# Mixing as three products of rounded and rest parts, by units of 256 columns, in the spectral stage of a two-layer kernel

## The reference, cut to what matters

```python
U_plus, U_minus = _stu_conv(phi, u, n)        # causal convolutions with each filter, of u and of u * (-1)^t
out = einsum('btkd,k,kde->bte', U_plus, s, Mpp) + einsum('btkd,k,kde->bte', U_minus, s, Mpm)
# once for each prefix T, T/2, T/4, T/8 with its own matrices; the four results are summed with weights
```

## Time and profile before

| | us |
|---|---|
| median of 3 runs (lowest, highest) | 6383.73 (6379.6, 6387.01) |
| profiled execution | 6381.82 |
| its span, first to last instruction | 6379.8 |
| PE busy in the span | 5717.1 (90%) |
| DVE, ACT, POOL busy | 4526.8, 3160.5, 2768.9 |

### The profile page before, as it was taken

How to read it: one execution, slowest core, us unless ns; L and a number is a source line. 1 busy time by engine, 2 the same in 40 slices (tenths; PEclk the granted TensorE clock), 3 DMA queues, 4 the chain that set the end, 5 groups by cost and what they waited for, 6 DMA issues and landing times. The chain is left out here.

```text
span 6379.8 us, 129054 instructions
## 1 busy us (share of the span) xinstructions
PE 5717.1 (90%) x41691; PEld 5077.2 (80%) x41691; DVE 4526.8 (71%) x6434; ACT 3160.5 (50%) x5994; POOL 2768.9 (43%) x1648
## 2 busy tenths in 40 slices
PE   7899999999789999999996537999999989999998
PEld 5688888888568888888874426888888878888887
DVE  2799999999629999999985654555555565556554
ACT  2799889988539988899873211111111111111110
POOL 1699999999429999999981000000000000000000
PEclk9899999999889999999998868999999999999999
DMA  2455555555315555555541037776766666767665
GB/s 95 111 145 144 140 140 144 143 143 139 118 51 148 141 142 143 141 142 141 139 135 57 27 99 168 154 149 143 148 146 149 148 166 146 150 149 152 152 150 141
DMA packets 1098935, 858.20 MB, mean 135 GB/s; under 512 B 305622, under 2 KB 1021238, under 8 KB 1064374
## 3 DMA queue, kind: packets, MB, share of 16 engines
q1 hardware_dynamic: 1097974, 844.72, 54.6%
q10 hardware_dynamic: 720, 10.49, 0.4%
HBM read 811.50 MB, written 43.55 MB: 134 GB/s over the span
## 5 line engine op out<-in xcount | busy, mean ns | idle before, releaser
L726 POOL TENSOR_TENSOR read<-state,c_wide 128x1024 f32<-128x1024 f32 x1024 | 2419.2, 2378 | 215.2 <-DVE state L762 127.7
L762 DVE TENSOR_TENSOR_SCAN state<-decay,carry,p_drive 128x512 f32<-128x512 f32 x1792 | 2140.6, 1258 | 103.8 <-PE p_drive L540 58.9
L658 ACT ACTIVATE decay<-step,a_neg 128x512 f32<-128x512 f32 x2048 | 1398.6, 718 | 224.8 <-DVE state L762 214.6
L1647 PE MATMUL p_y<-window,x_high 128*128 128x256 f32 x7936 | 1496.3, 286 | 0.0
L1711 ACT COPY term_blocks<-p_s 128x256 f32<-128x256 f32 x832 | 309.9, 372 | 2159.6 <-PE p_s L1647 2159.6
L1647 PEld LDWEIGHTS p_y<-window,x_high 128*128 128x128 f32 x7936 | 1244.7, 191 | 0.0
L1647 PE MATMUL p_y<-window,x_low 128*128 128x256 f32 x3968 | 1132.4, 285 | 0.0
L553 PE MATMUL p_y<-ident,read 128*128 128x128 f32 x8192 | 1064.1, 273 | 13.0 <-ACT y_tok L672 3.7
L542 PE MATMUL p_drive<-diag_b,xu_tok 128*128 128x128 f32 x8192 | 1004.0, 276 | 1.3 <-DVE state L762 1.3
L542 PEld LDWEIGHTS p_drive<-diag_b,xu_tok 128*128 128x128 f32 x8192 | 960.4, 193 | 1.6 <-DVE state L762 1.6
L553 PEld LDWEIGHTS p_y<-ident,read 128*128 128x128 f32 x8192 | 925.2, 141 | 25.4 <-issue 21.6
(11 more groups left out here) (249 smaller groups left out, 5424.0 us busy)
## 6 DMA issues: line engine op xcount, KB each, us to landing
c_wide<-c_scratch SPq DMA_DIRECT2D x256, 1024.0 KB, 4.8
window<-taps_scratch SPq DMA_DIRECT2D x576, 257.0 KB, 6.4
diag_b<-diag_scratch SPq DMA_DIRECT2D x256, 512.0 KB, 4.1
window<-taps_scratch SPq DMA_DIRECT2D x768, 129.0 KB, 5.0
window<-taps_scratch SPq DMA_DIRECT2D x128, 513.0 KB, 7.2
window<-taps_scratch SPq DMA_DIRECT2D x64, 385.0 KB, 6.0
gate_scratch<-gate_out SPq DMA_DIRECT2D x16, 512.0 KB, 3.1
gate_in<-gate_scratch SPq DMA_DIRECT2D x8, 1024.0 KB, 6.4
```

Of the source, the lines that this page charges most:

```text
L658: act.activation(decay[:, n % 2, t, :], step[:, c.parity, t, :], ACT.Exp, scale=m.a_neg[:, DT2 * c.k + t, n:n + 1]).then_inc(s["decay"], 1)
L726: pool.tensor_tensor(read[:, n % 4, :, :], state[:, n % 4, :, :], wide, ALU.mult).then_inc(s["read_out"], 1)
L762: dve.tensor_tensor_scan(flip(state[:, n % 4, t, :], c), flip(decay[:, n % 2, t, :], c), flip(p_drive[:, n % 2, t, :], c), 0.0 if c.start ...
L1647: last = pe.matmul(out, x[:, source, blk, :], view[:, :, at:at + P][:, :, ::-1], start=first and x is m.x_high and z == 0, stop=True, skip ...
```

## The change

The mixing's operands are split in a rounded part (fp32r) and the rest, as the convolution's are, and each fp32 matmul becomes three fp32r ones of 256 columns. A unit is one pair of slots (both parities, 256 columns); the 8 units of a pass are mixed after slots 15, 17, ... 27 and after slot 1 of the next pass. ACT makes the rounded part of each joined block (`round_filtered`, two slots behind its shared copies) and of the weights (`round_weights`, i = 7, 9), POOL the rest of both. `filtered` now has four places, one for each slot i modulo 4; `f_high` and `f_low` have one for each parity. The weights are scaled in place, which frees m_sum. The additions move behind the joins of slots 19, 23, 27. One block of the sources' differences is left out as unused (NBLK 41), and the second sequence's differences share one buffer for both sources.

```diff
--- before.py
+++ after.py
-BASE, DIFF, NBLK = 16, 28, 42
+BASE, DIFF, NBLK = 16, 28, 41
...
-        m_both, m_sum, mix_now = m.weights[:, 0:2], m.weights[:, 2], m.weights[:, 3:5]
-        blocks = sb("term_blocks", [P, 88, C])
+        m_both = m.weights[:, 0:2]
+        blocks = sb("term_blocks", [P, 76, C])
         terms = blocks[:, 0:48, :].rearrange("p (s i k h) c -> p s i k (h c)", s=2, i=6, k=2)
         shared = blocks[:, 48:56, :].rearrange("p (r k) c -> p r k c", k=2)
-        filtered = blocks[:, 56:88, :].rearrange("p (r s k h) c -> p r s k (h c)", r=2, s=2, k=2)
+        filtered = blocks[:, 56:72, :].rearrange("p (r k h) c -> p r k (h c)", r=4, k=2)
+        mix_now = [m.weights[:, 2], blocks[:, 72:76, :]]
+        f_high = sb("filtered_high", [P, 2, 2, NEAR], fp32r)
+        f_low = sb("filtered_low", [P, 2, 2, NEAR], fp32r)
+        mix_split = sb("mix_split", [P, 2, 2, FRACS, C], fp32r)
         u_next = [blocks[:, BASE * i:BASE * i + BASE, :] for i in range(2)]
-        d_next = [blocks[:, 2 * BASE + (NBLK - BASE) * i:2 * BASE + (NBLK - BASE) * (i + 1), :] for i in range(2)]
+        d_next = blocks[:, 2 * BASE:2 * BASE + (NBLK - BASE), :]
...
-            def mix(n, j):
-
+            def mix(n, u):
+
+                j, half = divmod(u, 2)
+                chunk = CHUNKS[j]
+                reach = MIX[chunk][half % len(MIX[chunk])][2]
+                cut = slice(half * NEAR, half * NEAR + NEAR)
                 for par in range(2):
-                    pe.wait_ge(s["added"], START + n * 8 + (2 * j + par - 1))
+                    if half == 0:
+                        pe.wait_ge(s["added"], START + n * 8 + (2 * j + par - 1))
                     if par == 0:
-                        pe.wait_ge(s["joined"], START + n * SLOTS + (16 + 4 * j))
-                    for at, size, reach in MIX[CHUNKS[j]]:
-                        for kind in range(2):
-                            last = pe.matmul(p_mix[par][:, at:at + size], mix_now[:, kind, reach, :],
-                                             filtered[:, j % 2, par ^ kind, kind, at:at + size], start=kind == 0,
-                                             stop=kind == 1)
-                    last.then_inc(s["mixed"], 1)
+                        pe.wait_ge(s["f_low"], START + n * 16 + (2 * u + 2))
+                    for kind in range(2):
+                        for w, f in ((0, f_high), (0, f_low), (1, f_high)):
+                            last = pe.matmul(p_mix[par][:, cut], mix_split[:, w, kind, reach, :], f[:, par ^ kind, kind, :],
+                                             start=kind == 0 and w == 0 and f is f_high, stop=kind == 1 and w == 1)
+                    if half == 1:
+                        last.then_inc(s["mixed"], 1)
+                    elif par == 1:
+                        last.then_inc(s["units"], 1)
             def body(n, k, first):
                 for i in range(SLOTS):
                     if i == 1 and not first:
-                        mix(n + -1, 3)
-                    if i == 17:
-                        pe.wait_ge(s["mix_now"], START + n * 2 + 2)
-                    if i in (17, 21, 25):
-                        mix(n, (i - 17) // 4)
+                        mix(n + -1, UNITS - 1)
+                    if i == 15:
+                        pe.wait_ge(s["m_low"], START + n * 2 + 2)
+                    if i >= 15 and i % 2:
+                        mix(n, (i - 15) // 2)
...
         def _(act):
+            def round_filtered(n, i):
+                act.wait_ge(s["joined"], START + n * SLOTS + (i + 1))
+                unit = (i - 12) // 2
+                if unit % 2:
+                    act.wait_ge(s["units"], START + n * 4 + (unit + 1) // 2)
+                else:
+                    act.wait_ge(s["mixed"], START + n * 8 + unit)
+                act.copy(f_high[:, i % 2, :, :], filtered[:, i % 4, :, :]).then_inc(s["f_high"], 1)
+
+            def round_weights(n, kind):
+                act.wait_ge(s["mix_now"], START + n * 2 + (kind + 1))
+                act.wait_ge(s["mixed"], START + n * 8)
+                act.copy(mix_split[:, 0, kind, :, :], mix_now[kind]).then_inc(s["m_high"], 1)
+
             def body(n, k, first):
                 for i in range(SLOTS):
                     if i // 2 != NO_SHARED:
                         act.wait_ge(s["shared_mm"], START + n * (SLOTS - 2) + (shared_before(i) + 1))
                         act.copy(shared[:, i % 4, :, :], shared_bank(i)).then_inc(s["kept"], 1)
+                    if i in (7, 9):
+                        round_weights(n, (i - 7) // 2)
+                    if i > 13:
+                        round_filtered(n, i - 2)
+                round_filtered(n, SLOTS - 2)
+                round_filtered(n, SLOTS - 1)
...
-            act.wait_ge(s["joined"], START + KF * SLOTS)
+            act.wait_ge(s["f_low"], START + KF * 16)
             act.dma_start(blocks[:, 0:2 * BASE, :], m.u_dram.rearrange("p s j c -> p (s j) c")).then_inc(s["u_in"], 16)
...
+        @block.gpsimd
+        def _(pool):
+            def body(n, k, first):
+                for kind in range(2):
+                    pool.wait_ge(s["m_high"], START + n * 2 + (kind + 1))
+                    pool.tensor_tensor(mix_split[:, 1, kind, :, :], mix_now[kind],
+                                       mix_split[:, 0, kind, :, :].bitcast(fp32), ALU.subtract).then_inc(s["m_low"], 1)
+                for i in range(12, SLOTS):
+                    pool.wait_ge(s["f_high"], START + n * 16 + (i - 11))
+                    pool.tensor_tensor(f_low[:, i % 2, :, :], filtered[:, i % 4, :, :],
+                                       f_high[:, i % 2, :, :].bitcast(fp32), ALU.subtract).then_inc(s["f_low"], 1)
+
+            for b in range(NB):
+                filters(pool, b, body)
...
                 if kind == 0:
                     dve.wait_ge(s["m_in"], START + n * 32 + 32)
-                else:
-                    dve.wait_ge(s["mix_now"], START + n * 2 + 1)
-                dve.tensor_tensor(m_sum[:, :, :], m_both[:, 0, :, :], m_both[:, 1, :, :],
+                    dve.wait_ge(s["m_low"], START + n * 2)
+                dve.tensor_tensor(mix_now[kind], m_both[:, 0, :, :], m_both[:, 1, :, :],
                                   ALU.subtract if kind else ALU.add).then_inc(s["built"], 1)
...
-                to = filtered[:, (g - 6) // 2 % 2, source, :, g % 2 * NEAR:g % 2 * NEAR + NEAR]
+                to = filtered[:, i % 4, :, :]
+                dve.wait_ge(s["f_low"], START + n * 16 + (i - 15))
...
-                    if i in (18, 22, 26):
-                        add(n, (i - 18) // 4)
+                    if i in (19, 23, 27):
+                        add(n, (i - 19) // 4)
...
                     for source in range(2):
-                        differences(dve, u_next[source], d_next[source], source, 1, diff)
-                    for source in range(2):
-                        keep_rest(dve, m, u_next[source], d_next[source], source, 1, high, low)
+                        if source:
+                            dve.wait_ge(low, START + 6)
+                        differences(dve, u_next[source], d_next, source, 1, diff)
+                        keep_rest(dve, m, u_next[source], d_next, source, 1, high, low)
```

More of the change, by code:

```diff
@@ L1233, in shared_before @@
     return i - min(max(i - 2 * NO_SHARED, 0), 2)
+UNITS = 8
 MIX = {0: [(0, 256, 3), (256, 256, 2)], 1: [(0, 512, 1)], 2: [(0, 512, 0)], 3: [(0, 512, 0)]}
@@ L1389, in differences @@
     pairs = rows.rearrange("p (g two) c -> p g two c", two=2)
-    dve.tensor_tensor(d[:, 12:20, :], pairs[:, :, 0], pairs[:, :, 1], ALU.subtract).then_inc(done, 1)
+    dve.tensor_tensor(d[:, 12:19, :], pairs[:, 0:7, 0], pairs[:, 0:7, 1], ALU.subtract).then_inc(done, 1)
     dve.wait_ge(done, START + 10 * b + 5 * source + 1)
@@ L1394, in differences @@
     pairs = d[:, 0:12, :].rearrange("p (g two) c -> p g two c", two=2)
-    dve.tensor_tensor(d[:, 20:26, :], pairs[:, :, 0], pairs[:, :, 1], ALU.subtract).then_inc(done, 1)
+    dve.tensor_tensor(d[:, 19:25, :], pairs[:, :, 0], pairs[:, :, 1], ALU.subtract).then_inc(done, 1)
 def round_sources(act, m, rows, d, source, b, diff, high):
@@ L1541, in spectral @@
         start_counts(nc, m.sem_x)
-        m.weights = sbk("mix_weights", [P, 5, FRACS, C])
+        m.weights = sbk("mix_weights", [P, LAGS, FRACS, C])
         m.recur = m.weights[:, 0:LAGS, :, :].rearrange("p l r c -> p (l r) c").rearrange("p (r l) c -> p r l c", l=LAGS)
@@ L1572, in filter_and_mix @@
         names = ["m_in", "m_read", "mix_now", "built", "shared_mm", "made", "kept", "joined", "terms",
-                 "merged", "mixed", "added", "acc_in", "acc_out", "u_in"]
+                 "merged", "mixed", "added", "acc_in", "acc_out", "u_in", "f_high", "f_low", "m_high", "m_low", "units"]
         s = {n: sem(n) for n in names + ["in_" + x for x in RUNS]}
@@ L1663, in slot @@
                         pe.wait_ge(s["in_" + half], START + n * 64 + 64)
```

(14 more changed lines are left out.)

## The result

The changed kernel takes 6647.28 us, median of 4 runs (6645.74 to 6647.76); the kernel before, run beside it, 6384.27. The ratio is 1.0412, with the interval 1.0394 to 1.043. The prediction was 6668, in a range from 6510 to 6740. The profiled execution took 6647.76 us with a span of 6646.0, so it stands 265.9 us above that of before. The granted clock was 0.963 over both.

What follows compares the result with a forecast made beforehand. PE's queue was taken as the path everywhere, so its waits count in full. A pass: -2.1 + 5.0 + 3.9 + 0.2 + 1.6 = +8.6 us; 32 passes, 275, plus 11 once gave 6668 us, range 6510 to 6740.

Steps and rivals of the forecast that it cites:

- products of the mixing: PE's mixing in a pass: 96 fp32r products, 11.7 us in place of 13.8, so 2.1 gained, at most 3.4.
- bank, units 2, 4, 6: After slots 19, 23, 27, PE waits for the addition that empties p_mix: 5.0 us lost a pass, bounds 4.5 to 5.4.
- parts, units 1, 3, 5, 7: PE waits at these units for ACT's rounding and POOL's rest, one place per source: 3.9 us lost a pass.
- parts, unit 0: Wait for the split parts at unit 0, where DVE is late with joins 12 and 13: 0.2 us, ends 0 and 0.6.
- weights, lock: POOL's weight subtractions hold off DVE's two-SBUF-input operations where PE waits for joins: 1.6 us lost a pass, ends 0 and 2.5.
- Once a run: Shared difference buffer delays rounding between the sequences, 5.9 us, and u_next loads about 5 later: 11 us in all.
- (a): Rival: in each pass the split is hidden, only the bank's wait is real: 2.9 us a pass, about 6486; chance 0.10.
- (b): Rival: waits in slots 23 to 1 make the clock fall, adding 10 us a pass: 7000 us; chance 0.07.
- (c): Rival: faster, bank and parts ready when PE arrives, a pass's waits under 2.1 us: 6273 to 6315; chance 0.04.
- (d): Rival: no change, a pass's waits and gain cancel within 0.4 us: 6384 us; chance 0.03.

Runs made afterwards that it cites:

- four moves: Changed kernel with additions one join earlier, weights made first, rounding ahead of the shared copy, rests of slots 22 and 23 by DVE: 6299.15 us, 0.9869.
- all moves: Changed kernel with additions earlier, weights first, rounding first: 6337.51 us, 0.993; second also with rests of slots 22 and 23 by DVE: 6299.15 us, 0.9869.

## Why the prediction was right

Sign, size and mechanism held: PE's queue is the path, and the waits in it add up. The terms of the sum, a pass:

| term | predicted | measured | from |
|---|---|---|---|
| products of the mixing | -2.1 | -2.3 + 0.7 | 0.119 apart; first of a unit 0.09 more |
| bank, units 2, 4, 6 | +5.0 | +4.9 | waits and tail |
| parts, units 1, 3, 5, 7 | +3.9 | +3.3 | waits and tail |
| parts, unit 0 | +0.2 | about 0 | no wait on a row |
| weights, lock | +1.6 | +1.4 | start of slot 2 (end of unit 7's mixing) to start of slot 12: 15.73 before, 17.17 after |
| sum | +8.6 | +8.0 | 8.02 between the passes |

**Products.** Unit 1 has no wait, so its rows on PE give the price alone (after):

```profile
4681.58 0.28 PE L1652 MATMUL p_y<-window,x_low 128*128 128x256 f32 x1
4681.70 0.38 PE L1695 MATMUL p_mix<-filtered_high,mix_split 128*128 128x256 f32 x1
4681.91 0.28 PE L1695 MATMUL p_mix<-filtered_low,mix_split 128*128 128x256 f32 x1
...
4683.10 0.28 PE L1695 MATMUL p_mix<-filtered_high,mix_split 128*128 128x256 f32 x1
4683.22 0.41 PE L1652 MATMUL p_s<-window,x_high 128*128 128x256 f32 x2
```

From 4681.91 to 4683.22 eleven products go by, 0.119 each: 96 of them 11.4 us against 13.8 before, 2.3 gained. The first takes 0.21 to the next, 0.09 more than the others; the eight units pay 0.07 to 0.11 each, 0.7 together, which I had not counted. Before, the extra stood at the other end. The prediction let the product behind the mixing start at 4571.91, two products before 4572.15, but its row starts earlier:

```profile
4571.72 0.59 PE L1647 MATMUL p_s<-window,x_high 128*128 128x256 f32 x2
```

So of the 3.44 that it gives a mixing, 3.26 are the mixing and 0.18 to 0.19 the change back to the convolution's products. The sum of the two, which the prediction used, is the same. The Trainium skill (TensorE: Matmul & The Clock Gate, Back-to-back issue gap) would have the product at 0.109 us; the row says 0.119, and the row stands.

**Bank.** Forecast 1.64, 1.64, 1.71; measured 1.61, 1.61, 1.68, and the run with earlier additions took 4.29 a pass away. DVE's rows for unit 2 in after are the chain that was added up: the join at 4692.19, both additions from 4692.80, PE at 4693.61:

```profile
4692.19 0.69 DVE L1818 TENSOR_TENSOR term_blocks<-p_y,term_blocks 128x512 f32<-128x512 f32 x1 [2.10 <-PE p_y L1652]
4692.80 1.47 DVE L1854 TENSOR_TENSOR acc<-acc,p_mix 128x512 f32<-128x512 f32 x2
```

**Parts.** Units 5 and 7 were put at 1.37 and cost 1.27 and 1.28. Unit 3 was put at 0.97 and cost 0.73, unit 1 at 0.24 and cost nothing. This is the term that was mis-sized. First PE, ACT and POOL at unit 5:

```profile
4711.35 0.28 PE L1695 MATMUL p_mix<-filtered_high,mix_split 128*128 128x256 f32 x1
```
```profile
4711.67 1.14 ACT L1726 CAST filtered_high<-term_blocks 128x512 fp32r<-128x512 f32 x2 [4.78 <-PE p_mix L1695]
```
```profile
4712.36 2.50 POOL L1767 TENSOR_TENSOR filtered_low<-term_blocks,filtered_high 128x512 fp32r<-128x512 f32 x2 [4.07 <-ACT filtered_high L1726]
```

POOL starts 0.69 behind ACT (forecast 0.62 + 0.08) and takes 2.50 for both blocks (forecast 1.27 + 1.24). But PE goes on at 4714.92, 0.06 behind POOL's end, where 0.15 had been put, taken from a wait for DVE: that is the 0.1 of the miss. Behind DVE it is indeed 0.12: at unit 2 the first of the two additions ends at 4693.49 and PE goes on at 4693.61.

Then ACT, DVE and POOL at unit 3, its second block:

```profile
4697.90 0.37 ACT L1737 COPY term_blocks<-p_s 128x256 f32<-128x256 f32 x1 [1.31 <-PE p_s L1652]
4698.17 0.62 ACT L1726 CAST filtered_high<-term_blocks 128x512 fp32r<-128x512 f32 x1
```
```profile
4698.31 0.42 DVE L1814 TENSOR_TENSOR term_blocks<-term_blocks 128x256 f32<-128x256 f32 x1
4698.65 0.42 DVE L1815 TENSOR_TENSOR term_blocks<-term_blocks 128x256 f32<-128x256 f32 x1
```
```profile
4698.87 1.32 POOL L1767 TENSOR_TENSOR filtered_low<-term_blocks,filtered_high 128x512 fp32r<-128x512 f32 x1 [0.87 <-ACT filtered_high L1726]
```

I had let POOL start when DVE's pair is done, at 4699.07. By its record it starts 0.20 earlier, behind ACT's rounding, which itself begins 0.27 behind the start of the shared copy. It then takes 1.32 in place of 1.27, and PE again goes on 0.06 behind its end (4700.19 to 4700.25). Together 0.20 - 0.05 + 0.09 = 0.24 less than forecast, which is the miss of unit 3 and, by the same chain, of unit 1. So the link before POOL is ACT's rounding; beside DVE's pair POOL was only 0.05 longer here.

**Weights.** Here the lock is about as large as forecast, once at each kind: 0.77 at the first, 0.68 at the second, where DVE's pair takes 1.96 in place of 1.28. After, POOL and DVE at the first kind, with DVE's 1.45 where the same operation takes 0.68 without company:

```profile
4653.87 1.27 POOL L1763 TENSOR_TENSOR mix_split<-mix_weights,mix_split 128x512 fp32r<-128x512 f32 x1 [10.05 <-ACT mix_split L1731]
...
4654.25 1.45 DVE L1780 TENSOR_TENSOR term_blocks<-mix_weights 128x512 f32<-128x512 f32 x1
```

It arrives at PE, which waits 0.62, 0.94 and 1.39 for the joins where it had waited twice (0.94, 0.70). In the run in which POOL subtracts 4 columns a pass takes 82.23, so 1.39 of the 1.44 came back.
The Trainium skill (SBUF — State Buffer, Who interferes with whom) calls the shared ports an exclusive lock and says that the order of issue decides who is blocked. DVE's 1.45 agrees: it started 0.38 behind POOL and took 0.77 longer, so it ended 0.56 behind POOL's end. In the run with late weights both are longer (1.84 and 2.36), although POOL's record starts 0.02 first. That would fit one operation of DVE's pair ahead of POOL and one behind it; the records do not show who held the port when.

**Once a run.** 9.3 us measured, 11 forecast: the wait for the first rounded parts rose by 3.9 (27.3 to 31.2), not 5.9. The other 5.4, where about 5 were put for the later load, are what is left over; no row shows them alone.

**Rivals.** (a), a hidden split, fell: with fp32 units and no split 2.74 a pass are gone. (b), a falling clock, did not happen in the changed kernel: its loop stands at 1.00. It did happen when some of its waits were removed (last section). Why the changed kernel was spared is not known, so in this point the forecast was also lucky. (c) needed waits under 2.1 a pass; they are 4.9 + 3.3 + 1.4 = 9.6. (d) needed sums that cancel; they differ by 8.0.

## What to carry to other kernels

An operation that empties a bank or fills a part must not stand behind the newest work of the engine that waits for it: behind joins 19, 23 and 27 the addition cost 1.6 to 1.7 us each time, one join earlier PE did not wait for it. Before splitting a product over helper engines, add up the helper chain (here 2.19 + 1.27 = 3.5 us for two blocks) against the queue's cover between two uses (2.2), and look for a stretch with room for each helper operation: the kernel with this split was 4.1% slower than before where its helpers were put first, and 1.3% faster after four moves. Where VectorE reads two SBUF inputs beside a GpSimd operation, ask which of the two the path waits for in that stretch: only there the delay counts.

## Unexpected of the hardware

In some runs with fewer waits the clock fell. One long window of the spectral loop, after first, then the runs with four places, with earlier additions, and with the rests by DVE:

```profile
3925.00:5095.00 1170.00, 1026.07 (x8112) 996.03 (x8111) 652.44 (x1340) 268.13 (x614) 324.56 (x251) 1.00 0.64 135
```
```profile
3925.00:5095.00 1170.00, 1060.22 (x8229) 1034.98 (x8228) 652.39 (x1350) 271.05 (x620) 330.61 (x254) 0.97 0.64 136
```
```profile
3925.00:5095.00 1170.00, 1081.51 (x8504) 1055.46 (x8503) 700.99 (x1387) 280.54 (x643) 345.05 (x264) 0.98 0.66 140
```
```profile
3925.00:5095.00 1170.00, 1057.07 (x8289) 1030.37 (x8288) 690.21 (x1412) 271.68 (x623) 262.66 (x200) 0.98 0.64 137
```

PE's busy time in them is higher than in after and yet the mean granted clock lower. In after, the same three waits for the joins stand in the same place and the clock stays at 1.00; in the run with four places it is at 0.50 behind them. So neither a wait by itself nor their number makes the fall. The clock did not fall in every faster kernel. The two with all moves, which have none of these three waits, are busier still and stay at 1.00 until the first sequence ends (the first row is the one without rests on DVE):

```profile
3925.00:5040.00 1115.00, 1076.44 (x8773) 1067.07 (x8773) 781.89 (x1446) 288.95 (x661) 354.37 (x271) 1.00 0.72 153
```
```profile
3925.00:5040.00 1115.00, 1094.15 (x8938) 1086.93 (x8938) 810.40 (x1493) 293.80 (x672) 323.80 (x246) 1.00 0.71 155
```

The run with weights first has none of the three either and is at 1.00, and so is the one with 4 columns, which has two. The four in which the clock fell (four places, earlier additions, rests by DVE, rounding first) all kept the three waits, as the changed kernel did. What decides stays open: no run varied one wait alone. Missing were 31 of 82 us with the four places and 19 of 137 with the earlier additions, of which 4.6 and 2.5 lie between the sequences; that the clock took the rest is argued from the windows, not shown.
The Trainium skill (TensorE: Matmul & The Clock Gate, A second HAM failure mode: psum-queue depth-cycling) knows of a kernel whose short idles made the clock go up and down; the rows of the four places agree, while those of after, with more idle time, do not.
